# Attention's row maxima: one reduction over 1024 keys from a double bank, with outputs and transposed maxima in the same ring

## What is computed

```
q, k, v = heads of (x @ w_qkv)            # 4 sequences x 16 heads, 1024 x 16 each
attn = softmax(q k^T / sqrt(16), axis=-1) # 1024 x 1024 for each head
y = attn v
```

## Time and profile before

| what | value |
|---|---|
| median of three runs | 1956.5 us (1955.85 to 1958.27) |
| the profiled execution's span | 1956.4 us |
| TensorE (PE) busy in it | 1666.7 us, 85% |
| VectorE (DVE) busy | 1365.5 us, 70% |
| ScalarE (ACT) busy | 1040.1 us, 53% |
| POOL busy | 329.0 us, 17% |
| the attention's first maximum matmul starts | 690.02 us |
| the attention's last value products start | 1488.60 us |

### The profile page before, as it was taken

One profiled execution on the slowest core, in us unless ns is written; L12 is line 12 of the kernel. 1 busy time (PEld: TensorE's weight loads), 2 busy tenths in 40 slices (PEclk: granted clock), 3 DMA queues, 4 the chain that ended last, 5 costly groups with the idle time before them and its releaser, 6 DMA issues. The chain is left out here.

```text
span 1956.4 us, 32665 instructions
## 1 busy us (share of the span) xinstructions
PE 1666.7 (85%) x9262; PEld 827.5 (42%) x9263; DVE 1365.5 (70%) x2360; ACT 1040.1 (53%) x1696; POOL 329.0 (17%) x390
## 2 busy tenths in 40 slices
PE   5028788888899689999999999999996856999997
PEld 5025555554445312232323332323223744666765
DVE  4879999996355278888888888888881761333332
ACT  2167787875344317777777777777774311222221
POOL 0043333230233300000000000000001571222222
PEclk9569999999899859999999999999998767999999
DMA  2010100011265453222232222222212442111110
GB/s 91 0 46 7 33 16 32 11 33 44 94 218 189 171 87 71 71 72 71 71 71 71 71 71 71 71 71 71 71 29 81 150 157 65 43 49 49 49 51 19
DMA packets 150085, 137.21 MB, mean 70 GB/s; under 512 B 67630, under 2 KB 123631, under 8 KB 150000
## 3 DMA queue, kind: packets, MB, share of 16 engines
q1 hardware_dynamic: 143952, 121.26, 22.6%
q0 software_dynamic: 5072, 14.77, 2.0%
q10 hardware_dynamic: 976, 0.24, 0.1%
HBM read 87.50 MB, written 49.23 MB: 70 GB/s over the span
## 5 line engine op out<-in xcount | busy, mean ns | idle before, releaser
L1208 DVE TENSOR_REDUCE at_mx<-at_pmx 128x1 f32<-128x512 f32 x1024 | 648.7, 682 | 78.2 <-PE at_pmx L1280 77.3
L1195 ACT ACTIVATE at_p<-at_pst 128x512 f32<-128x512 f32 x1024 | 539.6, 601 | 254.8 <-PE at_pst L1299 243.9
L1280 PE MATMUL at_pmx<-at_k,at_q 96*128 96x512 bf16 x1024 | 401.6, 394 | 15.1 <-DMA at_k<-scratch_ks 14.4
L1299 PE MATMUL at_pst<-at_q,at_k 99*128 99x512 bf16 x1024 | 354.1, 382 | 12.6 <-ACT at_p L1195 12.0
L1309 PE MATMUL at_pacc<-at_p,at_v 128*32 128x512 f32 x2048 | 273.6, 606 | 0.9 <-ACT at_p L1195 0.7
L497 ACT ACTIVATE ws_A<-ws_steps,par_beta,par_alpha 128x768 f32<-128x768 bf16 (+3 forms) x256 | 228.8, 962 | 44.6 <-PE ws_pA L634 29.6
L634 PE MATMUL ws_pA<-ident,ws_A 128*128 128x128 f32 x1408 | 193.4, 287 | 51.3 <-DVE ws_AT L585 36.8
L585 DVE TENSOR_TENSOR ws_AT<-ws_pA,ws_hitT 128x1024 f32<-128x1024 f32 (+1 forms) x192 | 213.3, 1128 | 9.6 <-PE ws_pA L634 9.3
L634 PEld LDWEIGHTS ws_pA<-ident,ws_A 128*128 128x128 f32 x1408 | 159.4, 146 | 131.0 <-DVE ws_AT L585 86.7
L1280 PEld LDWEIGHTS at_pmx<-at_k,at_q 96*128 96x128 bf16 x1024 | 99.9, 98 | 270.6 <-DVE at_mx L1208 195.9
L1299 PEld LDWEIGHTS at_pst<-at_q,at_k 99*128 99x128 bf16 x1024 | 99.6, 98 | 162.2 <-ACT at_p L1195 101.3
(11 more groups left out here) (229 smaller groups left out, 1747.0 us busy)
## 6 DMA issues: line engine op xcount, KB each, us to landing
w<-in_L_ffn_w SPq DMA_DIRECT2D x32, 512.0 KB, 4.7
at_q<-scratch_qs SPq DMA_DIRECT2D x192, 64.0 KB, 2.9
at_k<-scratch_ks SPq DMA_DIRECT2D x192, 64.0 KB, 3.0
scratch_v<-gp_v SPq DMA_DIRECT2D x8, 1024.0 KB, 5.7
at_v<-scratch_v SPq DMA_DIRECT2D x32, 256.0 KB, 3.6
scratch_qs<-gp_split SPq DMA_DIRECT2D x16, 384.0 KB, 2.7
scratch_ks<-gp_split SPq DMA_DIRECT2D x16, 384.0 KB, 3.4
ex_res<-scratch_routed SPq DMA_DIRECT2D x39, 130.0 KB, 2.3
```

The costliest lines, as they stand in the source:

```text
L1195: a.activation(pt[k // 2 % 4][:, k % 2, :], pst[bank(k)][:], ACT.Exp).then_inc(exped, 1)
L1208: v.reduce_max(mx[u % 2][:, m // 2, m % 2:m % 2 + 1], pmx[bank(m)][:], AX.X).then_inc(red, 1)
L1280: nc.tensor.matmul(pmx[bank(m)][:], qst[u][0:ROWS, h, nt * P:(nt + 1) * P], kst[u][0:ROWS, h, kh * HALF:(kh + 1) * HALF], start=True, stop ...
L1299: nc.tensor.matmul(pst[bank(k)][:], kst[u][:, h, t * P:(t + 1) * P], qst[u][:, h, p * HALF:(p + 1) * HALF], start=True, stop=True).then_in ...
```

## The change

The three single banks of the ring of maxima and the bank of the outputs become two double slots of two banks each. One M is now two matmuls, for the two halves of the keys, into the two banks of a slot, and one reduction over 1024 elements; there are 16 a unit, two in a step, and `tops` is gone. The outputs are transposed into the first bank of slot 1 (`OUT_SLOT`), the maxima into the first bank of slot 0 (`TOP_SLOT`). `slot` says which slot a maximum takes; at two places two neighbours share one, so that the other is free for the outputs (between maxima 10 and 11 of a unit) or for the transposed maxima. The order of a step is `SMSVSMS`, in step 1 `SMSSMSV`. `turn_tops` stands behind the first M of step 5 and waits for all maxima of the unit; `invert` and `normalise` stand together behind the first maximum of step 2; the links stand behind maxima 0 (two), 1 and 2. Maximum 12 waits for `normalise`, maximum 2 for the second link, maxima 1 and 11 for the maximum straight before them.

```diff
--- before.py
+++ after.py
@@ -1043,35 +1043,38 @@
     FULL = ROWS + 3
     HALF = L // 2
     PIECES = 2 * BT
-    MAXIMA = 2 * PIECES
+    MAXIMA = PIECES
     RING = 4
     PV0 = 2
     BANKS = 3
     LOADS = 2 * len(STACK) * 16
     TOPS = 4
     PER = MAXIMA // BT
-    ORDER = "SSMSMVMSM"
+    ORDER, LATE = "SMSVSMS", "SMSSMSV"
     TURN = 5
+    AHEAD = (BT - TURN) * PER
+    OUT_SLOT, TOP_SLOT = 1, 0
 
     qst = [sb(f"at_q{i}", [FULL, 2, L], BF16) for i in range(RING)]
     kst = [sb(f"at_k{i}", [FULL, 2, L], BF16) for i in range(RING)]
     vst = [sb(f"at_v{i}", [P, BT, 2, 2 * DK]) for i in range(RING)]
     pt = [sb(f"at_p{i}", [P, 2, HALF]) for i in range(4)]
-    mx, top_ = [sb(f"at_mx{i}", [P, PIECES, 2]) for i in range(2)], sb("at_top", [P, PIECES])
+    mx = [sb(f"at_mx{i}", [P, PIECES]) for i in range(2)]
     tail = sb("at_tail", [PIECES, P])
     top3 = [sb(f"at_top3{i}", [PIECES, 3, P], BF16) for i in range(2)]
     oe = sb("at_oe", [P, HALF])
     rden, yn = sb("at_rden", [P, 8, 2]), [sb(f"at_yn{i}", [P, 8, 2, 2 * DK]) for i in range(2)]
     pst = [ps(f"at_pst{i}", [P, HALF]) for i in range(BANKS)]
-    pmx = [ps(f"at_pmx{i}", [P, HALF]) for i in range(BANKS)]
-    pacc, pm = ps("at_pacc", [P, HALF]), ps("at_pm", [P, 8, 2, 2 * DK])
+    pmx = [ps(f"at_pmx{i}", [P, 2, HALF]) for i in range(2)]
+    pacc = ps("at_pacc", [P, HALF])
     one_rows = sem("at_ones")
     ld = [sem(f"at_load{i}") for i in range(RING)]
     v_in = [sem(f"at_v_in{i}") for i in range(RING)]
     scored, exped, pv, red, mxmm = (sem("at_" + n) for n in ("scored", "exp", "pv", "reduced", "maxima"))
-    topped, topT, split, rows_in, oed, oT, yd, rd = (sem("at_" + n) for n in ("top", "topT", "top_split", "top_rows", "acc_out", "outT", "y", "rden"))
+    topT, split, rows_in, oed, oT, yd, rd = (sem("at_" + n) for n in ("topT", "top_split", "top_rows", "acc_out", "outT", "y", "rden"))
     y_out = [sem(f"at_y_out{i}") for i in range(2)]
-    negT = pm[0:PIECES, 0:2, :, :].rearrange("p t h d -> p (t h d)")
+    pm = pmx[OUT_SLOT][:, 0, :].rearrange("p (t h d) -> p t h d", t=8, h=2)
+    negT = pmx[TOP_SLOT][0:PIECES, 0, 0:P]
 
     with nc.Block() as block, nc.allow_non_contiguous_dma(reason="per-channel vectors"):
         def bank(k):
@@ -1093,7 +1096,14 @@
 
         def early():
 
-            return [(0, 0, m) for m in range(MAXIMA)] + [(1, 1, m) for m in range((BT - TURN) * PER)]
+            return [(0, 0, m) for m in range(MAXIMA)] + [(1, 1, m) for m in range(AHEAD)]
+
+        def slot(w, m):
+
+            if isinstance(w, int) and w == 0:
+                return (m + 1) % 2
+            j = (m - AHEAD) % MAXIMA
+            return (j + (j > 4) + (j > 10)) % 2
 
         def turns(w):
 
@@ -1205,12 +1215,7 @@
 
             def maximum(w, u, m):
                 dve.wait_ge(mxmm, w * MAXIMA + m + 1)
-                v.reduce_max(mx[u % 2][:, m // 2, m % 2:m % 2 + 1], pmx[bank(m)][:], AX.X).then_inc(red, 1)
-
-            def tops(w, u):
-
-                dve.wait_ge(red, (w + 1) * MAXIMA)
-                v.tensor_tensor(top_[:], mx[u % 2][:, :, 0], mx[u % 2][:, :, 1], ALU.max).then_inc(topped, 1)
+                v.reduce_max(mx[u % 2][:, m:m + 1], pmx[slot(w, m)][:].rearrange("p a n -> p (a n)"), AX.X).then_inc(red, 1)
 
             def split_tops(w, u, link):
 
@@ -1247,24 +1252,19 @@
                     for n in range(PER):
                         if ms:
                             maximum(*ms[n])
-                        if s == 2 and not first:
-                            if n == 1:
-                                invert(w - 1)
-                            if n == 2:
-                                normalise(w - 1, i if u else i - 1, (u - 1) % RING)
+                        if s == 2 and n == 0 and not first:
+                            invert(w - 1)
+                            normalise(w - 1, i if u else i - 1, (u - 1) % RING)
                         if turns(w):
-                            if s == TURN - 1 and n == PER - 1:
-                                tops(w + 1, u + 1)
-                            link = (s - TURN) * PER + n - 1
-                            if 0 <= link < TOPS:
+                            for link in LINKS.get((s - TURN) * PER + n, ()):
                                 split_tops(w + 1, u + 1, link)
 
+            LINKS = {0: (0, 1), 1: (2,), 2: (3,)}
             for e in early():
                 maximum(*e)
-                if e[0] == 0 and e[2] == MAXIMA - 1:
-                    tops(0, 0)
-                if e[0] == 1 and e[2] < TOPS:
-                    split_tops(0, 0, e[2])
+                if e[0] == 1:
+                    for link in LINKS.get(e[2], ()):
+                        split_tops(0, 0, link)
             units(dve, unit)
             invert(UNITS - 1)
             normalise(UNITS - 1, UNITS // RING - 1, RING - 1)
@@ -1272,21 +1272,31 @@
         @block.tensor
         def _(pe):
             def maximum(w, u, m):
-                h, nt, kh = m // (2 * BT), m // 2 % BT, m % 2
+                h, nt = m // BT, m % BT
                 if m == 0:
                     pe.wait_ge(ld[u], (w // RING + 1) * LOADS)
-                if since(w, m) is not None:
-                    pe.wait_ge(red, since(w, m))
-                nc.tensor.matmul(pmx[bank(m)][:], qst[u][0:ROWS, h, nt * P:(nt + 1) * P],
-                                 kst[u][0:ROWS, h, kh * HALF:(kh + 1) * HALF], start=True, stop=True).then_inc(mxmm, 1)
-
-            def turn_tops(w):
-                pe.wait_ge(topped, w + 1)
-                nc.tensor.transpose(negT, top_[:], ident[:]).then_inc(topT, 1)
+                first, second = isinstance(w, int) and w == 0, isinstance(w, int) and w == 1
+                if m == 12 and not first:
+                    if not second:
+                        pe.wait_ge(yd, w - 1)
+                elif m == 2 and not first:
+                    pe.wait_ge(split, (w - 1) * TOPS + 2)
+                elif m in (1, 11) and not first:
+                    pe.wait_ge(red, w * MAXIMA + m)
+                elif not first or m >= 2:
+                    pe.wait_ge(red, w * MAXIMA + m - 1)
+                for kh in range(2):
+                    last = nc.tensor.matmul(pmx[slot(w, m)][:, kh, :], qst[u][0:ROWS, h, nt * P:(nt + 1) * P],
+                                            kst[u][0:ROWS, h, kh * HALF:(kh + 1) * HALF], start=True, stop=True)
+                last.then_inc(mxmm, 1)
+
+            def turn_tops(w, u):
+                pe.wait_ge(red, (w + 1) * MAXIMA)
+                nc.tensor.transpose(negT, mx[u % 2][:], ident[:]).then_inc(topT, 1)
 
             def turn_out(w):
                 pe.wait_ge(oed, w + 1)
-                pmf = pm[:].rearrange("p (t x) h d -> p t (x h d)", x=2)
+                pmf = pmx[OUT_SLOT][:, 0, :].rearrange("p (t n) -> p t n", t=4)
                 for t in range(4):
                     last = nc.tensor.transpose(pmf[:, t, :], oe[:, t * P:(t + 1) * P], ident[:])
                 last.then_inc(oT, 1)
@@ -1317,7 +1327,7 @@
                 for s in range(BT):
                     ms = beside(w, u, s)
                     k, n = 4 * s, 0
-                    for what in ORDER:
+                    for what in (LATE if s == 1 else ORDER):
                         if what == "S":
                             scores(w, u, k)
                             k += 1
@@ -1325,25 +1335,23 @@
                             if ms:
                                 maximum(*ms[n])
                             n += 1
+                            if n == 1 and s == TURN and turns(w):
+                                turn_tops(w + 1, u + 1)
                         elif what == "V":
                             if s:
                                 values(w, u, s - 1)
                             elif not first:
                                 values(w - 1, (u - 1) % RING, BT - 1)
                             if s == 2 and not first:
-                                if turns(w - 1):
-                                    pe.wait_ge(split, (w + 1) * TOPS)
+                                if ms:
+                                    pe.wait_ge(red, (w + 1) * MAXIMA + AHEAD + 4)
                                 turn_out(w - 1)
-                            if s == TURN and turns(w):
-                                if not first:
-                                    pe.wait_ge(yd, w)
-                                turn_tops(w + 1)
 
             pe.sem_inc(pv, PV0)
             for e in early():
                 maximum(*e)
-                if e[0] == 0 and e[2] == MAXIMA - 1:
-                    turn_tops(0)
+                if e[0] == 1 and e[2] == 0:
+                    turn_tops(0, 0)
             pe.wait_ge(one_rows, RING)
             units(pe, unit)
             values(UNITS - 1, RING - 1, BT - 1)
```

## The result

The changed kernel takes 1977.5 us (median of four runs, 1976.1 to 1978.6); the kernel before took 1956.2 beside it (four runs, 1955.3 to 1958.3). The ratio is 1.0105, with a 95% interval of 1.0091 to 1.0120: slower, by 18 to 23 us. The forecast was 1972.5, in a range of 1962 to 1981.

What follows compares the result with a forecast made beforehand. TensorE was taken as the bound: 23.32 us work plus .70 waiting per 24.02 us unit. The change makes 24.45, +.43 over 30 units; 12.9 + 1.6 + 1.8 - .4 = +15.9, so 1972.5 us, range 1962 to 1981.

Steps and rivals of the forecast that it cites:

- wide maximum: VectorE's reduction of 1024 from PSUM: 1.22 us, and 1.13 from one to the next.
- unit start: Score 0 of a unit waits for an exponential of the old unit; the wait of .41 becomes .19.
- step 1: Score 7 waits .30 for exponential 4, delayed by the accumulator's copy; the slot's wait for its maximum lies inside it.
- turn in step 5: Transpose of the maxima behind the first M waits for the unit's last wide maximum; score 21 starts .75 later.
- the .26 put in steps 3 and 4: Waits of maxima for VectorE while it also inverts and normalises, .26 a unit; the change removes them.
- rows landed before score 0: Rows of the maxima land before the next unit's score 0, hidden, with .2 to .3 left instead of .4 to .5.
- five loop ends, each: ScalarE stands still 2.24 at each loop end; such a unit costs about .3 more than now.
- a step without maxima: Last unit and a half, order S S V S S: 2.56 a step instead of 2.39, +1.8 over 11 steps.
- ahead of unit 0: Ahead of the loop VectorE sets the pace: -1.2 from wide maxima, +.8 from later links, -.4 in all.
- Faster: Rival: second matmul of a pair, same weights, follows sooner than .22; 1924 to 1952 us; chance .05 by the pair.
- Rows late too: Rival: wide maxima of 1.38 or landings of 2.1 make rows hold up each unit's start; 1980 us, chance .12.
- No difference: Rival: a wide maximum costs hardly more than a narrow one (.69), no wait at step 5; 1957 us, chance .05.

Runs made afterwards that it cites:

- e1: Changed kernel with the transpose of the maxima moved from behind the first M of step 5 to behind V of step 5: 1959.5 us, ratio 1.0015.
- e3: Changed kernel with each maximum taken over only the first 512 keys of its slot, the second half left out: 1953.7 us, ratio .9981.
- e8: Changed kernel with each wide maximum made as two narrow ones of 512 and a merge before the turn: 1985.5 us, ratio 1.0148.
- e2: Changed kernel with V one place earlier in step 1 (S MM S S V MM S): 1973.4 us, ratio 1.0093.
- e9: Kernel before with step 7 reordered to S S M S M V S M M, score 31 one matmul earlier: 1950.3 us, ratio .9963.
- e7: e6 with step 5 also in step 7's new order and S S S V S in steps without maxima: 1943.7 us, ratio .9934.
- e6: Changed kernel with e1's and e2's moves, step 7 as S MM S S V S MM, each row's DMA sent behind its link: 1945.3 us, ratio .9948.

## Why the prediction was right where it was, and where it was not

**The sum of the unit held**, and by its terms, not by chance:

| step of the prediction | predicted | measured |
|---|---|---|
| wide maximum | 1.22 | 1.219 |
| unit start | .19 | .20 |
| step 1 | .30 | .30 |
| outputs in slot 1 | 0 | 0 |
| turn in step 5 | .75 | .72 |
| the .26 put in steps 3 and 4 | -.26 | -.26 |
| unit | 24.45 | 24.43 |
| rows landed before score 0 | .2 to .3 | .25 to .27 |
| five loop ends, each | +.3 | +.23 |
| a step without maxima | 2.56 | 2.56 |
| ahead of unit 0 | -.4 | +.5 |

The turn's wait is also where the prediction said, and its cause is shown from three sides: moved behind V its wait goes (e1), with a shorter maximum it goes (e3), with a longer one it grows (e8).

**Step 1 was right in size and short of a cause.** I said that score 7's exponential sets the .30 and that the slot's wait "lies inside it". Both rows stand there one after the other, .18 for the slot and .12 for the exponential, behind the M. The sum is that of the later one, as predicted; but with the exponential alone out of the way at most .12 would come back. e2 shows the third that lies behind them, the copy.

**The .26 was right in size, wrong in place and cause.** I had put it in steps 3 and 4 and said that maxima wait there for VectorE "while it also inverts and normalises". The rows of before, TensorE's and then VectorE's, show it at the first two M of step 5, 5.4 us after `normalise` ended, with VectorE idle just before:

```profile
1025.43 0.60 PE L1299 MATMUL at_pst<-at_q,at_k 99*128 99x512 bf16 x2
1025.94 0.39 PE L1280 MATMUL at_pmx<-at_k,at_q 96*128 96x512 bf16 x1
...
1026.54 0.39 PE L1280 MATMUL at_pmx<-at_k,at_q 96*128 96x512 bf16 x1
```

```profile
1025.19 1.29 DVE L1208 TENSOR_REDUCE at_mx<-at_pmx 128x1 f32<-128x512 f32 x2 [0.36 <-PE at_pmx L1280]
```

Maxima 30 and 31 of a unit lie in banks 0 and 1, as scores 30 and 31 do, and maxima 0 and 1 of the next take the same banks, two later and not three. The M at 1025.94 waits for the maximum that ends at 1025.19 + .69 = 1025.88, the one at 1026.54 for the next. So this wait too came from how 32 fall on three banks. Whether another allotment of the single banks would win it in the kernel before, no run shows.

**The start** was mis-sized by .9. I had taken 1.13 from one wide maximum to the next, from rows at full clock. Ahead of the loop the clock is at .50, that is 1.2 GHz of 2.4 (a window of the changed kernel from the first maximum matmul until score 0: time, busy PE, PEld, DVE, ACT, POOL, clock, DMA), and six maxima in a row (VectorE's timeline) take 7.06:

```profile
691.00:719.00 28.00, 22.74 (x45) 3.25 (x45) 25.90 (x26) 0.00 (x0) 0.00 (x0) 0.50 0.64 77
```

```profile
699.43 7.06 DVE L1218 TENSOR_REDUCE at_mx<-at_pmx 128x1 f32<-128x1024 f32 x6
```

(7.06 - 1.22) / 5 is 1.17 from one to the next: with two slots and matmuls at half the clock, every second maximum waits for its data. And the first maximum starts 1.07 after the first M, behind two matmuls at half the clock, where a narrow one started .65 after it. The first row's DMA is issued 25.0 after the first M, where before it was 24.2.

**Unit 0 and the sum.** From score 0 to score 0 of the next, unit 0 takes 26.46 before and 25.23 in the changed kernel, 1.2 less, where I had counted .43 more. Windows of before, then of the changed kernel, from score 0 until the granted clock rises and behind (columns as above):

```profile
717.65:726.90 9.25, 9.25 (x27) 2.61 (x26) 6.28 (x11) 4.56 (x8) 0.00 (x0) 0.50 0.69 138
726.90:735.00 8.10, 8.10 (x47) 2.26 (x46) 6.76 (x12) 5.71 (x11) 0.00 (x0) 1.00 0.01 2
```

```profile
719.42:724.80 5.38, 5.38 (x13) 1.87 (x14) 3.31 (x4) 2.83 (x6) 0.00 (x0) 0.50 0.56 139
724.80:735.00 10.20, 10.20 (x60) 2.97 (x59) 7.86 (x7) 7.38 (x14) 0.00 (x0) 1.00 0.41 58
```

The clock stayed at .50 for 9.3 us of unit 0 before and for 5.4 after. That is not shown to be an effect of the change: in e9, which issues the same as the kernel before up to step 7, it rises 6.3 after score 0 and unit 0 takes 25.03, 1.4 less than before; over the twelve traces the point lies 3.4 to 9.3 behind score 0. Against the forecast, the attention then has +.9 at the start, +1.1 of late landings (next), -1.7 in unit 0, +.9 in the last two units (+2.8 where I had 1.8), -.5 at the loop ends and -.1 in all other units: +.7. So the unit was foreseen by its terms, but that the attention's 16.6 lies so near to the forecast's 15.9 is partly luck.

**Late rows** had a chance of .12 as the rule and none as the exception. The view of the rows' source line over the whole span, and over the start of unit 6 alone (their duration of issue is in the first line of each, the landing in the last):

```profile
DMA to landing us min/median/max: 1.6/1.7/2.6
```

```profile
L1145 SPq DMA_DIRECT2D at_q<-at_top x3: 514/589/590, 864.2 to 865.4; - x3
DMA to landing us min/median/max: 1.6/2.2/2.6
```

```profile
868.08 0.39 PE L1309 MATMUL at_pst<-at_q,at_k 99*128 99x512 bf16 x1 [0.75 <-ACT at_p L1205]
```

The third DMA, issued at 865.4, lands 2.6 later, at 868.0, and score 0 starts at 868.08, .71 late. The row names an exponential as what it waited for, but that had long been done: a wait for several things, put down to the wrong one. A second such landing, in unit 2, cost .42; the kernel before had one like it, its margin of .55 let .17 through to score 0, and the wait of its score 1 took that up: V to V is 24.02 there as elsewhere. That is +1.1, which the forecast lacks.

**The base.** I took the profiled span, 1956.4, for the median execution. In the changed kernel's runs the time lies 1.8 to 2.2 above the span. So the profiled execution of before was most likely the one of 1958.3, 2.1 above the median, and that of the changed kernel the one of 1976.1, 1.5 below: 17.9 + 2.1 + 1.5 = 21.5, the difference of the medians (21.4). A sum made against a span belongs on the time of that same execution, and carries the spread of a single run with it. By span the forecast's 15.9 stands against 16.6 for the attention; against medians it is 5 short. Of these 5 the traces place .7 in the attention (the sum above); 1.3 is the stretch ahead of the attention, which varies from run to run, and the remaining 3 or so I can only lay to the spread between single executions. Such a spread is there: the code outside the attention, the same in all twelve traces, takes 1154.5 to 1162.0 in them. That it makes these 3 was not shown.

**The rivals.** "Faster" hung on the second half of a pair coming sooner than .22. It came .22 after the first throughout. The section "Back-to-back issue gap" of "TensorE: Matmul & The Clock Gate" in the Trainium skill has about 131 ns as the sustained spacing of such a sequence; by this trace's rows, same weights or not, it is its other figure, 216 ns. "Rows late too" held in two units of 31. "No difference" was met in its unit, 23.90, when its condition was forced (e3).

## What to carry to other kernels

When an instruction is made wider to save on VectorE, follow its last occurrence before a join, not its sum: here 34 us less of VectorE's work cost 21 us, because the last maximum of a unit ended .5 later than a transpose asked for it, and moving that transpose by one V gave 18 of them back. Ask at each such wait what the engine could do first; the transpose moved, three steps in another order and rows sent earlier turned the change from 1% slower to .7% faster. And try the same reordering on the kernel before: a third of what the new ring seemed to promise was there to be had without it (e9), and another third, the .26, hung on which banks two maxima take.

## What the runs showed of the hardware that was not expected

- A reduction over 1024 fp32 elements in two PSUM banks takes 1.219 us by itself and 1.14 from one to the next; two of 512 take .686 and .679, or 1.29 from start to end. The second bank adds nothing that the rows show.
- The rows' DMAs, of 4 KB each, land after 1.7 in the median, but in ten of the twelve traces one to four of 96 take 2.1 to 3.6 (at most 2.1 before, 2.6 after, 3.6 in e7), in e6 and e9 none. They are rows of units 2 and 5 to 7, shortly before or after the loop's begin. What they collide with stayed open.
- At the end of each pass of the hardware loop ScalarE stands still for 2.0 to 2.2 us in the kernel before and 2.0 to 2.3 in the changed one, and a unit that holds one is 1.2 longer in the changed kernel and .95 in the kernel before. No experiment was made on this.
- The granted clock of TensorE rose from .50 to 1.00 at a point that lay 3.4 to 9.3 us behind score 0 in twelve traces, and 9.3 against 6.3 where two kernels had issued the same until then. Unit 0 was 1.4 us longer in the later case.
